# A two-layer transformer block on one core: statistics closed inside the stages, first attention begun with the first batch, writes and weights across stage borders

## The reference

```
x = x + window_attention(norm(x), W_qkv, W_out)        # 16 heads of 16, window 64, causal
x = x + mixture(norm(x), gate, 8 routed, 2 shared)     # top 2 of 8 SwiGLU experts + mean of 2 shared ones
x = x + attention(norm(x), wq..wo, gamma, beta)        # softmax over 256 groups, residual, own layer norm
x = x + routed_layer(norm(x), gate, experts)           # 8 Sinkhorn rounds, top 128 tokens for each expert
norm(x) = (x - mean(x)) / sqrt(var(x) + 1e-5)          # over the 256 features of a token
```

## Time and profile before

| | us |
|---|---|
| time before, median of 3 runs (2428.86 to 2436.8) | 2432.5 |
| the profiled execution, its own time | 2439.18 |
| its span in the trace | 2437.2 |
| PE busy (share of the span) | 2024.1 (83%) |
| DVE busy | 1630.2 (67%) |
| ACT busy | 1116.2 (46%) |
| POOL busy | 452.3 (19%) |

### The profile page before, as it was taken

One profiled execution on the slowest core, in us unless ns is written; L12 is line 12 of the kernel. 1 busy time (PEld: TensorE's weight loads), 2 busy tenths in 40 slices (PEclk: granted clock), 3 DMA queues, 4 the chain that ended last, 5 costly groups with the idle time before them and its releaser, 6 DMA issues. The chain is left out here.

```text
span 2437.2 us, 51300 instructions
## 1 busy us (share of the span) xinstructions
PE 2024.1 (83%) x18407; PEld 1393.6 (57%) x18408; DVE 1630.2 (67%) x2834; ACT 1116.2 (46%) x2169; POOL 452.3 (19%) x608
## 2 busy tenths in 40 slices
PE   2888888669979999989968899999999999835052
PEld 2766766448879999988857533434334343324042
DVE  3666666556735555546644579999999999386953
ACT  1555545333223333332223158888888888611010
POOL 2101001010011111114434112112221122030036
PEclk9999999889989999999989769999999999955566
DMA  2000000192151111113339777745755900031036
GB/s 87 2 0 0 0 0 0 60 336 80 35 182 47 47 47 47 47 43 106 109 114 271 201 51 72 67 46 52 49 47 47 71 2 2 5 104 35 0 112 200
DMA packets 207045, 172.15 MB, mean 71 GB/s; under 512 B 121740, under 2 KB 184808, under 8 KB 204744
## 3 DMA queue, kind: packets, MB, share of 16 engines
q1 hardware_dynamic: 187448, 131.64, 27.8%
q0 software_dynamic: 17744, 26.26, 4.0%
q10 hardware_dynamic: 1728, 12.58, 1.4%
HBM read 106.30 MB, written 63.84 MB: 70 GB/s over the span
## 5 line engine op out<-in xcount | busy, mean ns | idle before, releaser
L1811 DVE TENSOR_REDUCE ga_nmax<-banks 128x1 fp32r<-128x1024 f32 x512 | 615.5, 1219 | 39.8 <-PE banks L1890 38.4
L1845 ACT ACTIVATE ga_probT<-banks 128x512 f32<-128x512 f32 x1024 | 556.7, 597 | 157.6 <-PE banks L1903 105.9
L1890 PE MATMUL banks<-a_ks,a_qs 48*128 48x512 f32 x1024 | 392.3, 466 | 9.3 <-PEq L77 5.3
L1903 PE MATMUL banks<-a_qs,a_ks 49*128 49x512 f32 x1024 | 381.8, 453 | 0.0
L1920 PE MATMUL banks<-ga_probT,a_v 128*32 128x256 f32 x4096 | 332.9, 398 | 6.4 <-ACT ga_o L1851 6.4
L1890 PEld LDWEIGHTS banks<-a_ks,a_qs 48*128 48x128 f32 x1024 | 159.4, 195 | 225.2 <-DVE ga_nmax L1811 158.3
L1321 PEld LDWEIGHTS banks<-rb_xT,rb_own_w 128*128 128x128 f32 x2272 | 267.1, 193 | 8.3 <-issue 3.7
L1321 PE MATMUL banks<-rb_xT,rb_own_w 128*128 128x128 f32 x2272 | 267.9, 276 | 4.1 <-DMA rb_w<-in_L_ffn_rw_dram 3.5
L1790 POOL DMA_DIRECT2D a_qs<-ga_max_rows x256 | 130.8, 519 | 580.6 <-DVE ga_max_rows L1818 539.4
L1296 ACT ACTIVATE rb_silu<-banks,rb_own_b 128x128 f32<-128x128 f32 x284 | 80.9, 367 | 254.9 <-PE banks L1321 254.9
L1920 PEld LDWEIGHTS banks<-ga_probT,a_v 128*32 128x32 f32 x4096 | 81.6, 108 | 198.3 <-ACT ga_probT L1845 151.2
(11 more groups left out here) (288 smaller groups left out, 3031.7 us busy)
## 6 DMA issues: line engine op xcount, KB each, us to landing
m_xnT<-xnT_parts ACTq DMA_DIRECT2D x12, 1024.0 KB, 4.8
sorted_out<-rb_yb SPq DMA_DIRECT2D x71, 128.0 KB, 1.7
xnT_parts<-np_parts SPq DMA_DIRECT2D x8, 1024.0 KB, 9.2
m_w<-in_L_ffn_rw_dram SPq DMA_DIRECT2D x2, 4096.0 KB, 21.6
values<-pg_v SPq DMA_DIRECT2D x16, 512.0 KB, 3.1
a_v<-values SPq DMA_DIRECT2D x16, 512.0 KB, 9.1
a_qs<-queries_rounded SPq DMA_DIRECT2D x28, 256.0 KB, 8.5
a_ks<-keys_rounded SPq DMA_DIRECT2D x28, 256.0 KB, 9.6
```

Of the source, the lines that this page charges most:

```text
L1811: nc.vector.tensor_reduce(nmax[b % 2][:, at:at + 1], slot[:], axis=AX.X, op=ALU.max, negate=True).then_inc(use_read, 1)
L1845: nc.scalar.activation(probT[k % SETS][2 * h + n][:], b_t[ring_place["weights", w] % RING][:], ACT.Exp, scale=SCALE).then_inc(exp_ready, 1)
L1890: return nc.tensor.matmul(slot[:, HALF * kh:HALF * (kh + 1)], qs[a][rows, n, P * q:P * (q + 1)], ks[a][rows, n, HALF * kh:HALF * (kh + 1)] ...
L1903: nc.tensor.matmul(bank[:], ks[a][rows, 2 * gp + n, P * kt:P * (kt + 1)], qs[a][rows, 2 * gp + n, HALF * hf:HALF * (hf + 1)], start=True, ...
```

## The change

It does nine things:

1. The phases `setup` (its loads, identity and statistics) and ln0 are gone; their work is done inside `window_attention`.
2. There, SP loads batch 0, then W_qkv, then batches 1 to 3, then W_out. DVE takes the statistics of the 8 tiles of batch 0 and closes them (`finish(0, 0, TB)`) before the first normalisation. The other 24 tiles follow in step 0, four at each of the places 0 to 5, and are closed at place 6; ACT's root for them stands at place 7.
3. PE waits at first only for the identity; for the rest of W_qkv at the first product, for the constants and W_out at the first scores.
4. POOL builds the large mask by one copy from the small one instead of a memset and four selects.
5. ln1, ln2 and ln3 are gone; the same ten instructions (class `Closing`) stand at the head of DVE's and ACT's code in `normalised_tiles`, `project_groups` and `norm_residual`.
6. `normalised_tiles` writes its first two chunks straight into the tiles that the shared expert reads, so nothing is read back, and `parts` is a quarter smaller. Two of the shared experts' three weight buffers lie in a new tile that is kept for the whole kernel.
7. Its writes are no longer waited for at its end. Shared expert 0 waits for them: SP before it loads the routed weights, ACT before its first silu, DVE (for the rows) before its first gated product.
8. The weights and biases of `project_groups` are loaded in shared expert 1, into the new tile, after the shared weights in it are cut; the waits for them at the head of `project_groups` are gone.
9. The order of some SBUF tiles differs.

The diff, cut to its core:

```diff
+class Closing:
+
+
+    def __init__(self, nc, g, sb, sem):
+        self.nc, self.g = nc, g
+        self.diff, self.var, self.std, self.eps = sb("diff", [P, T]), sb("var", [P, T]), sb("std", [P, T]), sb("eps", [P, 1])
+        self.step, self.var_ready, self.std_ready, self.rstd_ready = [sem(n) for n in (
+            "stat_step", "var_ready", "std_ready", "rstd_ready")]
+
+    def on_vector(self, dve):
+        nc, g, link = self.nc, self.g, Chain(dve, self.step)
+        diff, var = self.diff, self.var
+        even, odd = g.stats[:, :, 1], g.stats[:, :, 4]
+        nc.vector.memset(self.eps[:], LN_EPS)
+        nc.vector.tensor_tensor(g.mean[:], even, odd, ALU.add)
+        nc.vector.tensor_tensor(var[:], g.stats[:, :, 2], g.stats[:, :, 5], ALU.add)
+        link(nc.vector.tensor_tensor(diff[:], even, odd, ALU.subtract))
+        link(nc.vector.scalar_tensor_tensor(diff[:], diff[:], D / 4.0, diff[:], ALU.mult, ALU.mult))
+        link(nc.vector.tensor_tensor(var[:], var[:], diff[:], ALU.add))
+        nc.vector.tensor_scalar(var[:], var[:], 1.0 / D, None, ALU.mult).then_inc(self.var_ready, 1)
+        link(nc.vector.tensor_scalar(g.mean[:], g.mean[:], 0.5, None, ALU.mult))
+        dve.wait_ge(self.std_ready, ONE + 1)
+        nc.vector.reciprocal(g.rstd[:], self.std[:]).then_inc(self.rstd_ready, 1)
+        dve.wait_ge(self.rstd_ready, ONE + 1)
...
+            def load_x(b):
+                src = g.ins["L0_attn_x"][b].rearrange("(t p) d -> p t d", p=P)
+                sp.dma_start(g.x[:, b * TB:(b + 1) * TB, :], src).then_inc(x_in[b], 16)
+
+            load_x(0)
             sp.dma_start(wqkv[:], g.ins["L0_attn_W_qkv"].rearrange("(k p) n -> p k n", p=P)).then_inc(wqkv_in, 16)
+            for b in range(1, B):
+                load_x(b)
...
-                for m, pat in ((mask0, [[0, NP]]), (mask1, [])):
-                    m = m[half(h)]
-                    link(nc.gpsimd.affine_select(out=m, in_=m, compare_op=ALU.is_ge, fill=NEG, base=WIN,
-                                                 pattern=pat + [[-1, W2]], channel_multiplier=1))
-                    link(nc.gpsimd.affine_select(out=m, in_=m, compare_op=ALU.is_ge, fill=NEG, base=-1,
-                                                 pattern=pat + [[1, W2]], channel_multiplier=-1))
+                m = mask1[half(h)]
+                link(nc.gpsimd.affine_select(out=m, in_=m, compare_op=ALU.is_ge, fill=NEG, base=WIN,
+                                             pattern=[[-1, W2]], channel_multiplier=1))
+                link(nc.gpsimd.affine_select(out=m, in_=m, compare_op=ALU.is_ge, fill=NEG, base=-1,
+                                             pattern=[[1, W2]], channel_multiplier=-1))
+            link(nc.gpsimd.tensor_copy(mask0[:], mask1[:].unsqueeze(1).broadcast_to([P, NP, W2])))
...
+            def tile_statistics(t):
+                if t % TB == 0:
+                    dve.wait_ge(x_in[t // TB], ONE + 16)
+                nc.vector.bn_stats(g.stats[:, t, :], g.x[:, t, :]).then_inc(tile_stats, 1)
...
+            nc.vector.memset(eps[:], LN_EPS)
+            for t in range(TB):
+                tile_statistics(t)
+            finish(0, 0, TB)
...
+                    if c == 0 and place < 6:
+                        for t in range(TB + 4 * place, TB + 4 * place + 4):
+                            tile_statistics(t)
+                    if c == 0 and place == 6:
+                        finish(1, TB, T)
...
+            def root(n, first, last):
+                act.wait_ge(var_ready, ONE + n + 1)
+                nc.scalar.activation(std[:, first:last], var[:, first:last], ACT.Sqrt, bias=eps[:, 0:1]).then_inc(std_ready, 1)
+
+            root(0, 0, TB)
...
+                        if c == 0 and place == UP - 1:
+                            root(1, TB, T)
...
-            pe.wait_ge(w_in, ONE + 16 * HU * 2)
-            pe.wait_ge(w_cut, ONE + 1)
-            pe.wait_ge(consts_set, ONE + 1)
+            pe.wait_ge(ident_set, ONE + 1)
...
+                    if first:
+                        pe.wait_ge(w_cut, ONE + 1)
...
+                    if c == 0:
+                        pe.wait_ge(consts_set, ONE + 1)
+                        pe.wait_ge(w_in, ONE + 16 * HU * 2)
...
+        part_of = lambda i: shared.xnT[i] if i < 2 else parts[:, :, :, C * P * (i - 2):C * P * (i - 1)]
...
-                if i == 5:
-                    sp.wait_ge(parts_kept, ONE + 16 * 4)
-                    for s in range(2):
-                        shared.load_chunk(sp, xnT_out, s, s, chunks_in)
                 if i:
                     sp.wait_ge(lo_ready, ONE + HALVES * i)
-                    sp.dma_start(xnT_out[i - 1], parts[:, :, :, C * P * (i - 1):C * P * i].bitcast(F32)).then_inc(parts_kept, 16)
+                    sp.dma_start(xnT_out[i - 1], part_of(i - 1)[:].bitcast(F32)).then_inc(parts_kept, 16)
             sp.wait_ge(lo_ready, ONE + HALVES * STEPS)
-            sp.dma_start(xnT_out[STEPS - 1], parts[:, :, :, C * P * (STEPS - 1):].bitcast(F32)).then_inc(parts_kept, 16)
+            sp.dma_start(xnT_out[STEPS - 1], part_of(STEPS - 1)[:].bitcast(F32)).then_inc(parts_kept, 16)
             sp.wait_ge(shared_in, ONE + 16 * shared.LOADS)
-            sp.wait_ge(chunks_in, ONE + 16 * 2)
-            sp.wait_ge(parts_kept, ONE + 16 * STEPS)
-            for u in range(2):
-                sp.wait_ge(rows_kept[u], ONE + 16 * (STEPS // 2))
...
+            if route is not None:
+                sp.wait_ge(shared.parts_kept, 16 * NC)
+                for kept in shared.rows_kept:
+                    sp.wait_ge(kept, 16 * NC // 2)
+            else:
+                sp.wait_ge(w_ready, ONE + 2)
+                project.load(sp, ins, routed_in)
+                sp.wait_ge(routed_in, ONE + 16 * project.LOADS)
...
+            for kept in shared.rows_kept:
+                dve.wait_ge(kept, 16 * NC // 2)
...
+            if route is not None:
+                act.wait_ge(shared.parts_kept, 16 * NC)
+                for kept in shared.rows_kept:
+                    act.wait_ge(kept, 16 * NC // 2)
...
+    def load(self, eng, ins, loaded):
+        for w, src in zip(self.w, (ins["L1_attn_wq"], ins["L1_attn_wk"], ins["L1_attn_wv"])):
+            eng.dma_start(w[:], src.rearrange("(k p) n -> p k n", p=P)).then_inc(loaded, 16)
+        for n, src in enumerate((ins["L1_attn_bq"], ins["L1_attn_bk"])):
+            for k in range(KD):
+                eng.dma_start(self.b_qk[:, n, k:k + 1], src[P * k:P * (k + 1)].rearrange("(p o) -> p o", o=1)).then_inc(loaded, 16)
+        bv_parts = ins["L1_attn_bv"].rearrange("(o q a d) -> a o q d", o=1, a=A, d=DH)
+        for a in range(A):
+            eng.dma_start(self.bv[a * GT:(a + 1) * GT], bv_parts[a].broadcast_to([GT, QT, DH])).then_inc(loaded, 16)
+        eng.dma_start(self.bo[:], ins["L1_attn_bo"].rearrange("(o n) -> o n", o=1).broadcast_to([P, D])).then_inc(loaded, 16)
...
-            pool.wait_ge(b_in, ONE + B_IN)
...
-            dve.wait_ge(b_in, ONE + B_IN)
-            dve.wait_ge(v_one, ONE + 2)
+            closing.on_vector(dve)
...
+            dve.wait_ge(v_one, ONE + 2)
...
-            act.wait_ge(b_in, ONE + B_IN)
+            closing.on_scalar(act)
...
-            pe.wait_ge(w_in, ONE + W_IN)
...
+            closing.on_vector(dve)
```

169 lines of the change are left out of this document (73 added, 96 removed).

## The result

The changed kernel takes 2393.97 us (median of 4 runs, 2391.57 to 2397.38) where the kernel before, beside it, takes 2434.65 (2428.86 to 2439.39): ratio 0.9841, 95% interval 0.9824 to 0.9858. The profiled execution took 2393.2 (span 2391.5), against the 2394.6 of the sum and the forecast of 2387.9 from the median. By the medians the change saves 40.7 us, where 44.6 were forecast. That the profiled execution came within 1.5 us of the sum is in part luck: the one profiled before took 2439.18, at the upper end of its range, and the terms missed in both directions.

What follows compares the result with a forecast made beforehand. Long stages run at PE's or DVE's own pace; the change touches four places where PE has nothing. 23.6 - 6.5 + 16.1 + 8.6 + 2.8 = 44.6 us saved: 2432.5 (median) to 2387.9, profiled 2439.2 to 2394.6; range 2374 to 2404.

Steps and rivals of the forecast that it cites:

- The start: Kernel start up to PE's first product: it comes at 20.9 in place of 44.46, saving 23.6 us (bounds 20 and 25).
- both covers: At the start, POOL's constants (near 13) and W_out (near 21) are ready before their users, so both cost nothing.
- Step 0: First window attention step: 24 statistics and their closing on DVE cost 6.5 us (bounds 2.4 and 13.5).
- Step 1 "as before": Second window attention step: length unchanged; a longer step 1 was named as a sign that the prediction was wrong.
- Into the mixture: Border from window attention to normalised_tiles: one small phase fewer, saving 2.7 us.
- Behind the normalising phase: Border to shared expert 0: first product 16.1 us earlier, 2.7 of it from the border before; 13.4 added here.
- the rival of the returning wait: Shared expert 0's first silu: writes end no earlier, PE stands 2.8 us, 2390.7 us in all; chance 15%.
- ACT's load of the third chunk: Shared expert 0: issued about 13 us sooner, among the routed weights, it takes some 5 us more; nothing lost.
- Projections: Head of project_groups: DVE starts 9.1 us earlier, less 0.5 lost beside POOL, saving 8.6 us.
- norm_residual: Head of norm_residual: gamma and beta asked for sooner, closing hidden under their wait, saving 2.8 us (bounds 0.7 and 3).
- the rival that more is saved where gaps shrink: Shared expert 0's first chunk: clock stays up, 2.6 us more, and 4 if step 0 hides its statistics: 2381; 18%.
- A switch of ACT's table: Start and step 0: rival that a switch blocks 1.4 us past its load, twice, giving 2390.7; chance 2%.

Runs made afterwards that it cites:

- p2: Changed kernel with glu padded before and behind in shared expert 0, and placed behind the weights with padding in shared expert 1: 2388.12 us, ratio 0.9815.
- u3: Changed kernel with the project_groups loads and their waits back at its own head, and phase ln3 back: 2427.24 us, ratio 0.9844.
- u2: Changed kernel with SP waiting for all row and part writes at the end of normalised_tiles, nothing read back: 2421.35 us, ratio 0.9823.
- u5: u2 with, besides, the wait for four written chunks and the reading back of the first two (2 MB): 2428.87 us, ratio 0.9884.
- u4: Changed kernel with the glu tiles allocated behind the weights again in shared expert 1 alone: 2421.76 us, ratio 0.9825.
- b1: Changed kernel with s4's edit and padding of 64 bytes ahead of glu and 192 behind in both shared experts: 2407.09 us, ratio 0.9769.
- s4: Changed kernel with step 0's 24 statistics at odd places only and ACT's root ahead of its transposed copy: 2391.1 us, ratio 0.9821.

## Why the prediction was right, step by step

**The start** was undersized by 1.5 us: the first DMA came 0.6 us, batch 0 1.2 and W_qkv 1.5 earlier than I had worked out from the earlier trace rows. The order of the chain was right, and both covers held. One term was missing: from the first product to the first maximum it is 8.96 us where it was 9.99. The products there took 0.41 us each up to 22.5 after the change and up to 50.0 before it, and 0.28 behind; these are the times that they also have at the lower and the higher level of the clock. So 1.0 us of the gain is the clock's.

**Step 0** was forecast at 6.5 and cost 29.38 - 23.76 = 5.6. It is less at the even places than the 4.1 of the sum: by the scores' times the pairs from place 0 to 4 lost 0.6 and 2.1, that from 4 to 6 nothing, and the last, with the closing, 2.5. But 4.4 us more of the step stood at the lower clock than before, and 6.1 of its 7.8 us lie in the pair from place 2 to 4. There the clock counts: the same code took 7.6 us in the changed kernel, and 6.8 in p2 with 4.2 at the lower level. So a part of the 2.1 that I had put down to DVE is PE's. In the pair from 0 to 2 it does not count: 6.44 us with 0.6 at the lower level in u3, and with 3.9 in u2. **Step 1 "as before" was wrong,** a longer step 1 being one of the signs against itself that the prediction had named: 1.9 us longer, by the clock, as the rows of its first pair show. The forecast treated the window attention's other steps as fixed. Together steps 0 and 1 cost 7.5.

**Into the mixture** 2.6 us by PE's first transposes (2.7 forecast). Behind it the last instruction stood 3.4 us earlier relative to the window attention, 0.7 more than forecast. **Behind the normalising phase** 13.8 for 13.4: right in size, and in its two causes by u2 and u5. The writes ended 496.12 - 489.66 = 6.5 us after the last instruction, 8.2 by the forecast, so the rival of the returning wait had even less room. ACT's load of the third chunk took 7.6 us from its issue at 511.22, inside the routed weights, and its later loads 4.7 to 5.0: 2.8 us more where some 5 were reckoned, and nothing waited for it.

**Projections** 8.4 for 8.6, **norm_residual** 2.0 for 2.8. The loads were issued 2.7 us earlier, nearly as forecast, but took longer: DVE's first rows came 5.2 us behind gamma's issue, 4.6 before. Both mechanisms stand by u3.

**What the sum did not have** nearly cancelled. Against the change: steps 1 and later in the window attention 2.7, and the two shared experts 3.6 (33.0 and 31.7 where 35.0 and 33.3 came in). Of these, 1.4 are shown to be the slower w3 products, by the seven chunks of p2. The first chunk of shared expert 0 lost the other 0.6. The 1.6 in shared expert 1 stay open, since u4 and b1 had the fast products there and chunks as long. The forecast named the tiles' order as a part of the change and gave it no price.

For the change: the 1.0 before the first maximum, 1.8 in the projections' loop and 2.6 in the group attention. The last two come with less time at the lower clock (5.6 for 10.3, and 75.8 for 84.3 up to norm_residual). They agree with the rival that more is saved where gaps shrink, but they are luck as far as is known: over the twelve kernels with this code from the projections' last rows to norm_residual it took 768 to 784 us. In the place where the rival put it, shared expert 0's first chunk, nothing came. That chunk took 14.00 us in place of 13.68, with the lower clock for 6.0 us of it, 5.4 before: the shorter gap did not keep the clock up there.

A switch of ACT's table blocks no longer than its load: 12.24 + 1.28 = 13.52 and the root starts at 13.54, and likewise at 52.30, 46.52 and 48.78. The rule of the Trainium skill (ScalarE: Activation LUTs, What ACT_TABLE_LOAD costs) of 2.66 us for a switch is not borne out here.

## What to carry to other kernels

Work put into a ring of three engines belongs where its engine waits anyway, and a table switch where ACT does: the same statistics made step 0 5.6 us longer spread evenly, a part of it by the clock, and 1.1 to 1.4 at the odd places with the root in ACT's gap. At a border of phases, ask of each wait and each transfer apart what it holds: here half was a wait whose user came later, and half 2 MB that need not be read at all. And compare the duration of the same product before and after whenever tiles have moved, since a total can be right while a slower inner loop and a lucky clock cancel. Then look at the loop's own length too: in one of the two experts here a faster product bought nothing.

## What was not expected of the hardware

**The offset of a tile in SBUF can change the time of a product.** 128x128 by 128x256 products in fp32 took 276 ns and their weight loads 188 where the two operands began at 32 and 224 modulo 256 bytes, and 283 and 192 where both began at the same offset (224, 32 or 0). In shared expert 0 that was 1.4 us over seven chunks (p2: 115.44, changed kernel: 116.8). In shared expert 1 no run shows a gain from it.

**What a us at the lower clock costs.** Over the twelve profiles up to p2 and s4, before and after among them, the rest of the window attention behind step 1 is the same code and lasts 366.5 to 371.0 us. Its time at the 1.2 GHz level was 17.3 to 31.7 us, and a straight line through the twelve gives 0.28 us for each (correlation 0.95; 0.93 with the two last profiles). PE is busy in 86% of it, but not all of that time is on the path. So a difference of 4 us between two kernels in such a stage needs no cause in the code.

**A small DVE operation beside POOL's memset.** In the closing of the projections the one-input operation of line 132 took 0.85 us in place of 0.18, at 1213.33 and in u3 at 1214.41 alike, and ended 0.03 to 0.04 us behind POOL's second memset of 128x1024 in all thirteen kernels that have it there. The five operations with two inputs before it took 0.19 to 0.21 us beside the same memsets.
